# A transformer layer on one core: a turned tile behind each burst of scores, and the branch turned round

## What is computed

```python
Q = (x @ Wq.T).reshape(b, n, H, R); K = ...; V = (x @ Wv.T).reshape(b, n, H, d)
attn = softmax(einsum('bnhr,bmhr->bhnm', Q, K))
x = layernorm(x + einsum('bhnm,bmhd->bnd', attn, V))
h = silu(tlin(x, w1)) * tlin(x, w2)
h = gelu(tlin(h, h1)); h = gelu(tlin(h, h2))
x = layernorm(x + tlin(h, w3))
```

## Time and profile before

| | us |
|---|---|
| median of 3 runs | 963.64 (963.21 to 964.0) |
| profiled execution, own time | 963.61 |
| its span, first to last instruction | 961.8 |
| TensorE busy | 948.4 |
| ScalarE busy | 849.2 |
| VectorE busy | 724.2 |
| GpSimd busy | 589.8 |

### The profile page before, as it was taken

How to read it: one execution, slowest core, us unless ns; L and a number is a source line. 1 busy time by engine, 2 the same in 40 slices (tenths; PEclk the granted TensorE clock), 3 DMA queues, 4 the chain that set the end, 5 groups by cost and what they waited for, 6 DMA issues and landing times.

```text
span 961.8 us, 19694 instructions
## 1 busy us (share of the span) xinstructions
PE 948.4 (99%) x6567; PEld 819.7 (85%) x6567; DVE 724.2 (75%) x1656; ACT 849.2 (88%) x2078; POOL 589.8 (61%) x590
## 2 busy tenths in 40 slices
PE   8999999999999999999999999999999999999997
PEld 6878888888888888888888888888888888888886
DVE  7988586786867778676886868868677786768757
ACT  7979999989989899898998999899898998989864
POOL 6944665746557475665746657465574756657654
PEclk9999999999999999999999999999999999999999
DMA  6000000100001000000000001000010000000000
GB/s 197 12 14 13 12 12 1 34 2 23 12 1 34 1 23 13 12 24 1 24 12 22 13 2 34 2 23 12 1 34 1 23 12 9 15 1 22 2 12 23
DMA packets 22053, 17.81 MB, mean 19 GB/s; under 512 B 1088, under 2 KB 18496, under 8 KB 21952
## 3 DMA queue, kind: packets, MB, share of 16 engines
q1 hardware_dynamic: 21952, 16.53, 5.6%
HBM read 12.33 MB, written 4.19 MB: 17 GB/s over the span
## 4 chain that ended last, share of the span: by engine, by line
PE 95%; DVE 2%; POOL 1%; issue 1%; DMA 0%; ACT 0%; SPq 0%; POOLq 0%; DVEq 0%; ACTq 0%
PE bank L1457 14%; PE bank L1580 13%; PE bank L1581 13%; PE bank L1451 13%; PE bank L1453 12%; PE bank L1452 12%; PE bank L1511 11%; PE bank L1560 3%; PE bank L1561 3%; PE bank L1640 1%; PE bank L1641 1%; DMA wq_in<-in_wq_t 0%; DVE neg_max L982 0%; DVE t_lo L277 0%; DVE v_lo L277 0%
## 5 line engine op out<-in xcount | busy, mean ns | idle before, releaser
L343 POOL TENSOR_TENSOR prob<-prob,inv_total 128x512 f32<-128x512 f32 x256 | 264.7, 1043 | 91.6 <-DVE inv_total L988 89.5
L561 ACT ACTIVATE prob<-bank,neg_max 128x256 f32<-128x256 f32 x512 | 238.1, 479 | 39.5 <-DVE neg_max L982 39.1
L277 DVE TENSOR_TENSOR pt_lo<-bank,pt_hi 128x512 fp32r<-128x512 f32 x256 | 171.8, 682 | 21.6 <-ACT pt_hi L280 20.6
L982 DVE TENSOR_REDUCE neg_max<-bank 128x2 f32<-128x512 f32 x256 | 170.4, 678 | 19.4 <-PE bank L1511 18.8
L277 DVE TENSOR_TENSOR v_lo<-bank,v_hi 128x512 fp32r<-128x512 f32 x128 | 87.4, 683 | 109.7 <-ACT v_hi L280 108.6
L280 ACT ACTIVATE pt_hi<-bank 128x512 fp32r<-128x512 f32 x256 | 151.6, 612 | 17.9 <-PE bank L1457 17.6
L277 POOL TENSOR_TENSOR odd_lo<-gated,odd_hi 128x512 fp32r<-128x512 f32 (+1 forms) x66 | 82.0, 1243 | 132.3 <-ACT odd_hi L280 128.5
L1451 PE MATMUL bank<-pt_hi,v_hi 128*128 128x256 f32 x512 | 153.4, 300 | 0.0
L1457 PE MATMUL bank<-ident,prob 128*128 128x128 f32 x1024 | 151.4, 273 | 1.9 <-POOL prob L343 1.5
L1457 PEld LDWEIGHTS bank<-ident,prob 128*128 128x128 f32 x1024 | 123.1, 141 | 28.5 <-POOL prob L343 1.9
L1453 PE MATMUL bank<-pt_hi,v_lo 128*128 128x256 f32 x512 | 144.4, 282 | 0.0
(11 more groups left out here) (147 smaller groups left out, 2358.9 us busy)
## 6 DMA issues: line engine op xcount, KB each, us to landing
xt_in<-in_x_t SPq DMA_DIRECT2D x16, 256.0 KB, 2.6
res<-in_x SPq DMA_DIRECT2D x16, 256.0 KB, 2.7
out_x<-y SPq DMA_DIRECT2D x15, 256.0 KB, 2.3
h_in<-in_h_t SPq DMA_DIRECT2D x2, 1024.0 KB, 8.9
w_in<-in_w_t SPq DMA_DIRECT2D x3, 256.0 KB, 5.6
wv_in<-in_wv_t SPq DMA_DIRECT2D x1, 512.0 KB, 4.7
out_x<-y SPq DMA_DIRECT2D x2, 128.0 KB, 1.8
wq_in<-in_wq_t SPq DMA_DIRECT2D x1, 192.0 KB, 3.8
```

What stands on the lines that cost most here:

```text
L277: return eng.tensor_tensor(dst, src, hi.bitcast(F32), ALU.subtract)
L343: nc.gpsimd.tensor_tensor(prob[:, s, :, :], prob[:, s, :, :], inv_total[:, u, :].unsqueeze(2).to_broadcast([P, NT, N]), ALU.mult).then_inc ...
L561: last = nc.scalar.activation(prob[:, slot(i, u, RING), nt, :], sc_bank(i, u)[:, nt * N:(nt + 1) * N], ACT.Exp, bias=neg_max[:, u, nt:nt + 1],
L982: nc.vector.tensor_reduce(neg_max[:, u, :], sc_bank(i, u).rearrange("p (t m) -> p t m", m=N), AX.X, ALU.max, negate=True).then_inc(s_max, 1)
```

## The change

The order of all engines is written anew, in front of the branch, in the cycle and in `last`, with new bank tables. The operations are the same, with these exceptions: VectorE adds a comparison `is_equal` to the flag, so that the exact copy is the body of the `If` and the other copy the `Else`; the high part of `wqa` goes from GpSimd to ScalarE, that of `wqb` and of the `x` of pair 1 from ScalarE to GpSimd; the low part of `wv0` goes from VectorE to GpSimd, that of `wka` the other way; `halves` goes to the end of VectorE's first part; the last norm goes into `res` in place of `y` and takes its `var_eps` from VectorE; some copies of the last halves change between ScalarE and VectorE. In front of the branch stands now also what was the first half of `cycle(1)`, down to `times_v(1, 3)`, and `cycle` starts its second half with `layer1_z1(k - 1, 0)`.

The bursts of scores and what TensorE does next:

| where | before | after |
|---|---|---|
| first part | 11 bursts: 10 before other work, 1 before a turned tile | 10 bursts: 5 before other work, 5 before a turned tile |
| cycle, groups 3 to 5 | `times_v` | `turn_x1` |
| cycle, groups 6 and 7 | `layer1_z2` | `turn_prob(k, 9)` |
| cycle, groups 0 and 1 of the next pair | `turn_prob(k, 12)` | `turn_prob(k, 12)` |
| cycle, group 2 of the next pair | `times_v` | `turn_prob(k + 1, 0)`, or `turn_attention` in `last` |
| `last` | 4 bursts: 3 before other work, 1 before a turned tile | 3 bursts: 1 before other work, 2 before a turned tile |

The core of the diff; the rest reorders the same calls.

```diff
@@ -299,7 +299,7 @@
             def store_half(b):
                 sp.wait_ge(s_y, LAST + b + 1)
                 t = slice(b * NT, (b + 1) * NT)
-                sp.dma_start(out_rows[LAST][:, t, :], y[:, t, :]).then_inc(s_yfree, 16)
+                sp.dma_start(out_rows[LAST][:, t, :], res[:, t, :]).then_inc(s_yfree, 16)
 
             sp.dma_start(xt_in[:, :], x_t[0]).then_inc(s_xin, 16)
             sp.dma_start(wq_in[:, A], wq_t[:, A]).then_inc(loads["wqa"], 16)
...
             def rstd2_half(b):
-                rstd(LAST, slice(b * NT, (b + 1) * NT), (after(LAST, TT, (b + 1) * NT), LAST + b + 1),
-                     mv2, var_eps2, rstd2, s_mv2, s_ve2, s_rs2)
-
-            weight_high("wqa")
+                t = slice(b * NT, (b + 1) * NT)
+                pool.wait_ge(s_veh, b + 1)
+                nc.gpsimd.tensor_tensor(rstd2[:, t], var_eps2[:, t], minus_half[:, t], ALU.pow).then_inc(s_rs2, 1)
+
             weight_low("wqa")
-            weight_low("wka")
+            weight_high("wqb")
             weight_high("wv0")
+            weight_low("wv0")
+            xt_high(1)
             weight_low("wv1")
...
             xt_high(0)
+            weight_high("wqa")
             weight_high("wka")
-            weight_high("wqb")
             t_high(0, 0)
...
                 tanh(k - 1, 2)
                 high(k - 1, 1, 1)
+                pt_high(k, 7)
+                pt_high(k, 8)
                 t_high(k + 1, 3)
+                v_high(k, 6)
                 exp(k, 12)
                 exp(k, 13)
-                exp(k, 14)
                 pt_high(k, 9)
                 acc_copy(k, 0)
+                exp(k, 14)
+                tanh(k - 1, 3)
                 pt_high(k, 10)
                 exp(k, 15)
...
                 dve.wait_ge(s_flagt, 1)
                 nc.vector.tensor_reduce(lo_flag[0:1, 0:1], FLAG_BANK[0:1, 0:P], AX.X, ALU.max).then_inc(s_flag, 1)
+                dve.wait_ge(s_flag, 1)
+                nc.vector.tensor_scalar(lo_flag[0:1, 1:2], lo_flag[0:1, 0:1], 0.0, None, ALU.is_equal).then_inc(s_flag, 1)
 
             def halves():
                 dve.wait_ge(s_scales, 16)
...
             def stats2_half(b):
+                t = slice(NT * b, NT * (b + 1))
                 stats(LAST, sum2_half(b), tiles_of(b), stats2, mv2, s_yadd, LAST + b + 1, s_st2, s_mv2)
+                dve.wait_ge(s_mv2, after(LAST, TT, NT * (b + 1)))
+                nc.vector.tensor_scalar(var_eps2[:, t], mv2[:, t, 1], EPS, None, ALU.add).then_inc(s_veh, 1)
 
             def norm2_half(b):
-                need(dve, s_yfree, 16 * LAST)
                 hold(dve, s_rs2, LAST + b + 1)
-                norm(y, sum2_half(b), tiles_of(b), mv2, rstd2).then_inc(s_y, 1)
+                norm(res, sum2_half(b), tiles_of(b), mv2, rstd2).then_inc(s_y, 1)
 
             xt_low(0)
+            weight_low("wka")
             weight_low("wqb")
+            weight_low("wkb")
             t_low(0, 0)
-            weight_low("wkb")
...
             def cycle(k, w):
                 if k > 1:
-                    turn_prob(k, 0, (s_pt_lo, k - 1, J, 15))
-                    turn_y(k - 3, (s_gelu2, k - 2, KC, 4))
-                    layer3(k - 2, 0, 0, w, (s_v_lo, k, VT, 2))
-                    layer3(k - 2, 1, 0, w, (s_pt_lo, k - 1, J, 16))
+                    turn_prob(k, 0, (s_gelu2, k - 2, KC, 2))
+                    times_v(k - 1, 12)
+                    layer2(k - 2, 3, 1, w)
+                    times_v(k - 1, 13)
+                    turn_prob(k, 1, (s_t_lo, k, H, 7))
+                    values(k, 1, (s_gelu2, k - 2, KC, 3))
+                    turn_y(k - 3, (s_pt_lo, k, J, 1))
...
+                    layer3(k - 2, 3, 1, w)
+                    scores(k, 3, (s_pt_lo, k, J, 3), (s_gelu3, k - 2, KC, 3))
+                    scores(k, 4, (s_x1, k - 1, 2, 2), (s_v_lo, k, VT, 4))
+                    scores(k, 5, (s_pt_lo, k, J, 4), (s_gelu3, k - 2, KC, 4))
+                    turn_x1(k - 1, (s_v_lo, k, VT, 5))
+                    times_v(k, 0)
+                    times_v(k, 1)
+                    times_v(k, 2)
+                    turn_prob(k, 4, (s_exp, k, J, 7))
+                    times_v(k, 3)
+                    layer4(k - 2, 0, w, (s_exp, k, J, 8))
+                layer1_z1(k - 1, 0, w, (s_x1t_lo, k - 1, 1, 1))
+                layer4(k - 2, 1, w)
+                turn_prob(k, 5, (s_exp, k, J, 10))
+                layer1_z1(k - 1, 1, w, (s_exp, k, J, 9))
+                layer1_z2(k - 1, 0, w, (s_pt_lo, k, J, 5))
+                times_v(k, 4)
                 if k == 1:
-                    scores(k, 4, (s_v_lo, k, VT, 5), (s_v_lo, k, VT, 2))
+                    query_or_key(k + 1, 0, (s_exp, k, J, 8))
...
-                scores(k, 6, (s_pt_lo, k, J, 8), (s_t_lo, k + 1, H, 1))
-                scores(k, 7, (s_t_lo, k + 1, H, 2), (s_t_lo, k + 1, H, 3))
-                layer1_z2(k - 1, 2, w, (s_silu, k - 1, KC, 3))
...
+                query_or_key(k + 1, 3, (s_v_lo, k, VT, 6))
+                scores(k, 6, (s_silu, k - 1, KC, 3), (s_t_lo, k + 1, H, 2))
+                scores(k, 7, (s_t_lo, k + 1, H, 3), (s_pt_lo, k, J, 8))
+                turn_prob(k, 9, (s_pt_lo, k, J, 9))
                 times_v(k, 6)
                 times_v(k, 7)
-                turn_prob(k, 9, (s_t_lo, k + 1, H, 4))
...
-                scores(k + 1, 0, (s_exp, k, J, 16), (s_silu, k - 1, KC, 4))
-                scores(k + 1, 1, (s_pt_lo, k, J, 12), (s_pt_lo, k, J, 10))
-                turn_prob(k, 12, (s_t_lo, k + 1, H, 5))
...
+                scores(k + 1, 0, (s_silu, k - 1, KC, 4), (s_gate, k - 1, KC, 4))
+                scores(k + 1, 1, (s_t_lo, k + 1, H, 5), (s_exp, k, J, 16))
+                turn_prob(k, 12, (s_gate, k - 1, KC, 3))
...
-                scores(k + 1, 2, (s_gelu2, k - 1, KC, 3), (s_v_lo, k + 1, VT, 1))
-                times_v(k, 13)
+                scores(k + 1, 2, (s_exp, k + 1, J, 3), (s_pt_lo, k, J, 14))
 
...
-                turn_y_half(1, (s_gelu3, 15, KC, 4))
+                turn_y_half(1, (s_y, 14, 1, 1))
...
+            turn_prob(1, 4, (s_exp, 1, J, 7))
+            times_v(1, 3)
             pe.wait_ge(s_halves, 2)
-            pe.wait_ge(s_flag, 1)
-            any_lo = pe.value_load(lo_flag[0:1, 0:1].bitcast(I32))
-            with pe.If(any_lo):
+            pe.wait_ge(s_flag, 2)
+            all_exact = pe.value_load(lo_flag[0:1, 1:2].bitcast(I32))
+            with pe.If(all_exact):
+                for k in range(1, LAST):
+                    cycle(k, False)
+                last(False)
+            with pe.Else():
                 for k in range(1, LAST):
                     cycle(k, True)
                 last(True)
-            with pe.Else():
-                for k in range(1, LAST):
-                    cycle(k, False)
-                last(False)
 
```

More of the change, by code:

```diff
@@ new lines, in _ @@
+            pt_low(0, 6)
+            row_max(0, 13)
+            v_low(0, 6)
+            t_low(1, 2)
+            inverse(0, 10)
+            largest_low(5)
+            inverse(0, 11)
+            pt_low(0, 7)
+            largest_low(6)
+            inverse(0, 12)
+            row_max(0, 14)
+            v_low(0, 7)
+            row_max(0, 15)
+            pt_low(0, 8)
+            t_low(1, 3)
+            t_low(1, 4)
+            pt_low(0, 9)
+            largest_low(7)
+            inverse(0, 13)
@@ new lines, in _ @@
+            inverse(0, 14)
+            row_max(1, 0)
+            inverse(0, 15)
+            row_max(1, 1)
+            largest_low(8)
+            pt_low(0, 10)
+            largest_low(9)
+            row_max(1, 2)
+            pt_low(0, 11)
+            largest_low(10)
+            row_max(1, 3)
+            flag_by_partition()
+            pt_low(0, 12)
+            inverse(1, 0)
+            v_low(1, 0)
+            pt_low(0, 13)
+            t_low(1, 5)
+            inverse(1, 1)
+            pt_low(0, 14)
@@ new lines, in last @@
+                turn_prob(15, 5, (s_exp, 15, J, 8))
+                turn_prob(15, 6, (s_x1, 14, 2, 2))
+                layer1_z1(14, 0, w, (s_exp, 15, J, 9))
+                values(15, 4, (s_x1t_lo, 14, 1, 1))
+                times_v(15, 4)
+                layer1_z1(14, 1, w, (s_pt_lo, 15, J, 6))
+                times_v(15, 5)
+                scores(15, 5, (s_exp, 15, J, 10), (s_pt_lo, 15, J, 5))
+                turn_prob(15, 7, (s_gelu3, 13, KC, 4))
+                layer1_z2(14, 0, w, (s_silu, 14, KC, 1))
@@ new lines, in last @@
+                times_v(15, 6)
+                layer4(13, 0, w, (s_pt_lo, 15, J, 7))
+                layer1_z2(14, 1, w, (s_silu, 14, KC, 2))
+                layer4(13, 1, w)
+                layer1_z1(14, 2, w, (s_gate, 14, KC, 1))
+                values(15, 5, (s_gate, 14, KC, 2))
+                layer1_z2(14, 2, w, (s_v_lo, 15, VT, 5))
+                layer1_z1(14, 3, w, (s_pt_lo, 15, J, 8))
+                scores(15, 6, (s_yt, 13, 1, 1), (s_exp, 15, J, 11))
```

(31 more changed lines are left out.)

1160 lines of the change are left out of this document (546 added, 614 removed).

## The result

| | before | after |
|---|---|---|
| median on one chip, 20 runs each | 963.85 (963.04 to 966.68) | 961.98 (961.01 to 963.04) |
| ratio, 95% interval | | 0.9976 (0.997 to 0.9983) |
| profiled execution: span | 961.8 | 959.8 |
| last matmul starts at | 955.74 | 952.28 |
| one cycle | 58.520 | 58.480 |

Faster, by 1.9 us and not by 6.1. The median lies outside the range of 955.0 to 960.8.

A forecast was written before the change was run, and what follows sets the result against it. The prediction took TensorE's own order as the bound, busy 99%, with VectorE setting the start. Terms 2.9 + 1.5 + 1.2 + 0.4 + 0.1 = 6.1 us, from 963.6 to 957.5 us, range 955.0 to 960.8.

The forecast's parts named there:

- Leaving a burst: Exits from score bursts cost 0.045 us less when a turned tile follows; 47 exits get cheaper, 2.1 us gained.
- the two bursts fewer: Score bursts fall from 71 to 69, each saving entry and exit of 0.19 us: 0.8 us gained.
- rival 3: At the score bursts, the drain is the same whatever follows: 2.1 us lost, 959.6 us; chance 0.07.
- Bank tables and other orders in the cycle: New bank tables and reordered ScalarE, VectorE and GpSimd queues hold the same operations, covered by TensorE's backlog: costed at nothing.
- rival 2: One TensorE wait per cycle, tightest at times_v(k, 8) on ScalarE's copy; 965.9 us at 0.6 us each; chance 0.16.
- The branch: TensorE's 1.52 us idle at the compare-and-branch goes because the exact copy falls through: 1.5 us gained, bounds 0 and 1.5.
- Rival 1: The branch gives nothing: falling through stalls as long, or the wait was GpSimd's; 1.5 and 0.4 us lost, 959.4 us; chance 0.12.
- The start: VectorE, which sets 9 to 20 us, is relieved: 1.2 us gained; less TensorE idling behind the branch, 0.4 us.
- rival 4: Start waits elsewhere, on GpSimd's later low parts: 1.2 + 0.4 us less, 1 us more at the ends, 960.1 us; chance 0.07.
- The end: Last norms into `res` and `var_eps` of the last halves from GpSimd to VectorE: net 0.1 us gained.
- 3.5 us would end near 959.1, under the last stores: The jump now at the end of the exact copy follows TensorE's last transposes and is hidden, with cover of 2.7 us.
- `last`: New order of the final part: no gain taken; TensorE's waits for `yt`, 1.0 us, bound gain or loss.

The follow-up runs named there:

- e5: Kernel before the change with scores(k + 1, 2) moved ahead of turn_attention(k, 0), one exit per cycle: 964.37 us, ratio 0.9994, cycle 58.467 for 58.520 us.
- e6: Kernel before the change with its seven working PSUM banks renamed by a fixed permutation, nothing else: cycle 58.520 us.
- e10: Changed kernel with its PSUM banks renamed by a fixed permutation, nothing else: cycle 58.480 us.
- e4: Kernel before the change with only the branch turned round, exact copy as body of the If: 964.94 us, ratio 1.0012.
- e8: On top of e3, VectorE takes t_low(0, 6) and (0, 7) before weight maxima, GpSimd normalises tiles 1 and 2 before weight_low(2): 961.19 us, 0.996.
- e7: On top of e3, pair 1 alone gets another order of copies, high and low parts on ScalarE and VectorE: 960.29 us, 0.9951.
- e11: On top of e7, each maximum over the weights' low parts reads 8 columns, leaving out part of the check: 960.15 us, 0.9957.
- e3: Changed kernel with one wait for VectorE's last addition, so TensorE jumps later at the end of the exact copy: 960.28 us, 0.9957.
- e1: Changed kernel with the branch the old way round, low-parts copy as body of the If: 963.55 us, ratio 0.9988.

## Why the prediction was wrong

- **Leaving a burst, 2.1 us, and the two bursts fewer, 0.8 us: right.** 2.8 to 3.0 us measured for 2.9. Counted as in the forecast, over all bursts, an exit is 0.195 us before products or layer 1 and 0.148 before a turned tile, an entry 0.197. e5 shows it in isolation, which rules out rival 3. The Trainium skill, "TensorEngine Tiling (Array Packing)", Key Properties, has the drain at a change of mode without exception; the measured exits differ by what follows.
- **Bank tables and other orders in the cycle, nothing: wrong by 0.10 us a cycle.** The cycle was to lose 0.14 us and lost 0.04: 58.520 before (the forecast has 58.51), 58.480 after. I had set the pitches of ordinary matmuls as given. They came out longer in the cycles, 1.4 us in 14 of them; over the whole run it is 0.7 to 1.2 us by the two sortings. The loss came with the order, not with the banks (e6, e10) and not with a wait (809.00 of 809 us busy, so rival 2 is out as well). The cause below that is open.
- **The branch, 1.5 us: the record was read rightly, the gain was mis-sized.** It falls through in 0.083 us. But a gap is not a gain where others are late: in e4 VectorE's `t_lo` and `pt_lo` took back 0.5 of the 1.5 us. Rival 1, that nothing comes of it, was a third right.
- **The start, 1.2 + 0.4 us: this is the step that failed first.** I took VectorE's relief as TensorE's. VectorE stayed as full (10.69 of 11 us for 10.93), its queue now has three maxima of weights in this stretch where it had two, two of them ahead of low parts that TensorE waits for, and beside it stand GpSimd's tiles and the loads (e8, and ScalarE's `weight_high(1)`, a term that the forecast did not have). Of 3.1 us forecast for branch, start and the stretch behind it, all waits together gave 1.2 to 1.8. That is rival 4, set at 0.07 and priced too low: it met the branch's gain as well, which I had kept apart. The waits of 0.96 and 0.92 us in pair 1 are new ones of the new order (e7, e11).
- **The end, 0.1 us: wrong by 1.5 us and in sign.** "3.5 us would end near 959.1, under the last stores" counted the jump as TensorE's time alone, and as that it is hidden: TensorE is done with it at 956.1. What it fetches goes over the DMA engines that carry the last store. I had the fetch in the earlier trace rows and did not move it along. e3 takes 1.6 us back. The gain of the new `var_eps` on VectorE and of `res` is there (last matmul to issue of the last store 3.80 us for 3.89), as small as forecast.
- **`last`, nothing: about right.** Its waits are 1.7 us for 1.5 (1.0 for `yt` and 0.5 for a bank of layer 1 that VectorE still read).
- With the bursts, pitches and waits of the table and the end as forecast the sum is 3.0 - 0.7 + 1.2 + 0.1 = 3.6 us; e3, which has the end right, gains 3.8 us (960.28 for 964.12).

The Trainium skill's "Runtime: NRT & Kernel Launch", Instruction fetch mechanics, gave the fetch at a jump out of the loaded window, and the runs agree: 3.3 to 4.2 us for the jump in all thirteen traces that have one, and packets of 16 KB. The 108 ns of "Advanced Engine Details and Errata", Control Flow Timing, in the Trainium skill is near the branch that falls through, 0.083 us, and not the one that jumps.

## What to carry to other kernels

When TensorE's stall is taken away, ask for the two waits that stood in its shadow before counting it; here a gap of 1.5 us was worth 1.0, and the rest of the start could not be had from one engine's relief. A jump moved to the end of a kernel is not free because its engine has finished: what it fetches shares the DMA engines with the last stores. And a burst of 64-row matmuls is left 0.05 us cheaper into transposes than into products, which can be summed by count; but in a loop the distances of the other matmuls can move with the order by as much (here 0.10 of 0.14 us a cycle), so measure the cycle.

## What the runs showed of the hardware

- **Instruction packets hold up tensor DMAs.** One packet of 16 KB is recorded at 0.88 to 1.93 us over all traces, 1.26 us in the one that meets the last store after the change. The store's packets of 512 bytes behind that one, 0.03 us each before it, are recorded at 0.05 to 0.08 us.
- **A jump can cost the clock too.** In e1 the gap of 1.95 us was followed by 3.4 us at 0.50 to 0.53. The gap of 1.52 us in the kernel before was followed by none of it (1.00), nor was one of 2.34 us in the profile of e6, where the next matmuls have their usual pitch. So the length of a gap alone does not foretell it.
- **Two small VectorE instructions can take 1.2 us each.** The profile of e6 (966.52 us, and the kernel before has times like it, up to 966.84) has `half_s`, 0.15 us in the earlier trace rows, so:

```profile
11.92 1.22 DVE L958 TENSOR_SCALAR half_s<-scales 128x4 f32<-128x4 f32 x1
13.17 1.18 DVE L960 TENSOR_TENSOR half_s<-half_s,scales 128x4 f32<-128x4 f32 x1
...
15.73 0.50 PE L1474 MATMUL bank<-xt_hi,wk_hi 128*128 128x512 f32 x1 [2.34 <-DVE t_lo L278]
```

TensorE waits 2.34 us for it. The change moves `halves` away from the start, and none of its 20 runs was over 963.04. That the one is the cause of the other was not tried.
